# Two windowed-attention layers on one core: set-up cut into pieces with a semaphore each, and rel banks of 6, 4 and 4 image rows

## The chip, the cores and the metric

The kernel runs on one core of a Trainium2 chip. The time is the device time of one execution in microseconds (us). The engines are called as in the profile: PE (TensorE; PEld are its weight loads), DVE (VectorE), ACT (ScalarE), POOL (GpSimd) and SP (SyncE, whose queue SPq issues all transfers here).

## The reference

x is (64, 14, 14, 192). Two layers follow each other, each `x = x + attention(groupnorm(x))`, with 32 channel groups per sample and no affine part. Attention has 12 heads of 16 channels over the 196 tokens of a sample, with decomposed relative positions added to the scores:

```
attn = (q * 16**-0.5) @ k.T
attn[h, w, kh, kw] += q . Rh[h, kh] + q . Rw[w, kw]
out = softmax(attn) @ v @ proj_w + proj_b
```

Rh and Rw are rows of two tables of 27 x 16 per layer, picked by the difference of the two rows or columns of the image.

## The kernel before, in words

A unit is one sample of one layer; there are 128. Each engine runs the same loop of passes (`iteration`, line 500 for PE, 696 for DVE) with twelve slots each. A step of unit u is due at a fixed slot count after the unit's start (`JOBS`, lines 255 to 266, with the PSUM bank of each job), so up to nine units are in work at once: in each slot PE makes the row-maximum product of one head of one unit (line 511), the score product of one head of an older unit (line 524), and the jobs due there. All order within an engine is the order of this program, and engines meet through semaphores only. The passes are numbered i from -2; unit n has its step "at" in pass n + at // 12, slot at % 12.

The steps of a unit: the tile xa of a sample is loaded (line 386), PE transposes it (`xT`, line 421), ACT copies it, DVE takes channel statistics (line 726), PE sums them over groups with the matrix gmat (`g`, line 427), DVE copies the sums (line 771), POOL makes mean and rstd and the normalized xn, split into two half-precision parts xn_hi and xn_lo (lines 799 to 831). PE multiplies by split weights w_hi and w_lo (line 404) to q, k (`qk0`, `qk1`) and v (`v`). q and k go out to DRAM and come back in the layout of q_st and k_st.

The relative positions are extra rows of the contraction. k_st holds, in its rows 64 to 124, one-hot rows for image row, image column and a row of constants, the same for all heads and units (line 658 copies them head by head into six buffers). q_st gets, by transfer, the products of q with the tables (`rel0` to `rel2`, line 465). These are made for RELB = (6, 6, 2) image rows at a time, one PSUM bank for each: for each of 14 columns or rows i two small matmuls for the column axis, and for i below the number of image rows in the bank two more for the row axis. ACT writes the first part of each bank (line 619), DVE the rest (line 756). rel0 uses bank 0 in slot 5, rel1 bank 2 in slot 6, rel2 bank 2 in slot 8; V's product of another unit uses bank 2 in slot 9 and waits for rel2's reader on DVE (`bank_free`, line 289). After rel2, SP issues four transfers (line 355).

After the maxima of all heads (DVE, line 705), `mT` in slot 5 of a later pass turns them, ACT writes mrow, SP sends it to q_st (line 346), and the first score product needs it in slot 9. ACT takes the exponential (line 574). PE multiplies with V in groups of four heads, in slots 2, 5 and 8 (line 543); the group of slot 8 needs the exponential of the score product of the same slot. The rest (`ot`, `oT`, `y`) normalizes, projects and adds the residual (POOL, line 841).

Set-up: SP issues all constant transfers, then the weights of layer 0 and, after these are split, those of layer 1 through the same buffer w_raw (line 323). DVE fills pads (lines 643 to 651), makes the one-hot rows of all six k_st buffers, the pick table, the rel table rel_st, and scales and splits both layers' weights (lines 653 to 691). Then it signals s_setup; PE, ACT and POOL wait for that before their first instruction (lines 395, 553, 780).

Of the kernel before, what the change touches and what calls it, by code (L numbers as in the profile page):

```python
# [56 lines left out]
RELB = (6, 6, 2)  # L57
# [17 lines left out]
def attention_kernel(nc, x_in, w_all, b_qk, b_rows, rel, onehot, lo_rows, ident_in, gmat_in, out):  # L75
    with ExitStack() as ctx:
        def sb(name, shape, dt=F32):
            return ctx.enter_context(nc.sbuf_tensor(name, shape, dt))
# [19 lines left out]
        w_raw = sb("w_raw", [CB, 2, 4 * C])  # L98
# [59 lines left out]

        s_const = sem("s_const")
        s_wraw = sems("s_wraw", 2)  # L160
        s_pad = sem("s_pad")
        s_wsc = sem("s_wsc")
        s_bhi = sem("s_bhi")
        s_whi = sem("s_whi")
        s_wlo = sem("s_wlo")
        s_oh = sem("s_oh")
        s_setup = sem("s_setup")
# [143 lines left out]
        def _(sp):  # L311
            sp.dma_start(ident[:, :], ident_in).then_inc(s_const, 16)
            sp.dma_start(gmat[:, :], gmat_in).then_inc(s_const, 16)
            sp.dma_start(oh_raw[R_REL:STACK, :], onehot).then_inc(s_const, 16)
            sp.dma_start(is_lo[:, :], lo_rows).then_inc(s_const, 16)
            for part in range(2):
                sp.dma_start(b_raw[CC + part:CC + part + 1, :, :, :], b_qk.rearrange("(o n) l t -> o n l t", o=1))\
                  .then_inc(s_const, 16)
            for l in range(2):
                sp.dma_start(rel_in[2 * HD * l:2 * HD * l + 2 * HD, :, :, :],  # L320
                             rel[0:2 * HD].rearrange("(r d) l a n -> d r (l a n)", d=HD)).then_inc(s_const, 16)
            for layer in range(LAYERS):
                if layer:
                    sp.wait_ge(s_wlo, layer)
                sp.dma_start(w_raw[0:CC, :, :], w_all[layer].rearrange("(c p) n -> p c n", c=2))\
                  .then_inc(s_wraw[layer], 16)
# [14 lines left out]
            def iteration(unit, layer):  # L341
                for s in range(HEADS):
# [51 lines left out]
        def _(pe):  # L394
            pe.wait_ge(s_setup, 1)
            pe.wait_ge(s_const, 16 * 8)
# [12 lines left out]
            def job(name, unit, slot, layer):  # L409
# [14 lines left out]
                elif name == "g":  # L424
                    pe.wait_ge(s_mv, u.n + 1)
# [3 lines left out]
                elif name.startswith("qk"):  # L429
                    pe.wait_ge(s_xlo, u.n + 1)  # L430
# [68 lines left out]

            def iteration(unit, layer):  # L500
                for s in range(HEADS):
# [139 lines left out]
        def _(dve):  # L641

            nc.vector.memset(rel_raw[:, :, :, :], 0.0).then_inc(s_pad, 1)
            nc.vector.memset(halfpow[:, :], -0.5)
            nc.vector.memset(eps[:, :], EPS)
            nc.vector.memset(w_raw[CC:CB, 1, :], 0.0).then_inc(s_pad, 1)
# [3 lines left out]
            for i in range(VB):  # L650
                nc.vector.memset(v_st[i][:, :, :, :], VS)
            dve.wait_ge(s_const, 16 * 8)
            nc.vector.tensor_copy(oh_f16[R_REL:STACK, :].rearrange("p (k b r) -> p k r b", r=2, b=SIDE),
                                  oh_raw[R_REL:STACK, :].rearrange("p (k r b) -> p k r b", r=2, b=SIDE)).then_inc(s_oh, 1)
            dve.wait_ge(s_oh, 1)
            for i in range(QB):
                for head in range(HEADS):
                    nc.vector.tensor_copy(k_st[i][R_REL:STACK, head, :], oh_f16[R_REL:STACK, :])  # L658
            used = HG * (HD + 1)
            by_head = ident[:, :].rearrange("p (j x) -> p j x", x=PW)  # L660
            nc.vector.tensor_copy(pick[:, 0:used].rearrange("p (j x) -> p j x", j=HG), by_head[:, :, 0:HD + 1])
            nc.vector.tensor_copy(pick[:, used:128].rearrange("p (j x) -> p j x", j=HG), by_head[:, :, HD + 1:PW])
            dve.wait_ge(s_pad, 1)
            nc.vector.tensor_scalar(rel_raw[:, :, :, 0:2 * REL], rel_in[:, :, :, :], RS, None, ALU.mult)\
              .then_inc(s_wsc, 1)
            dve.wait_ge(s_wsc, 1)
            nc.vector.tensor_copy(rel_st[:, :, :, :], rel_raw[:, :, :, :]).then_inc(s_whi, 1)
            dve.wait_ge(s_whi, 1)
            nc.vector.tensor_scalar(rel_cut[:, :, :, :], rel_st[:, :, :, :], is_lo[0:64, 0:1], None, ALU.mult)\
              .then_inc(s_whi, 1)  # L670
            dve.wait_ge(s_whi, 2)
            nc.vector.tensor_tensor(rel_st[:, :, :, :], rel_raw[:, :, :, :], rel_cut[:, :, :, :], ALU.subtract)
            for layer in range(LAYERS):
                dve.wait_ge(s_wraw[layer], 16 * 3)
                dve.wait_ge(s_pad, 2)
                w_qk = w_raw[:, :, 0:2 * C].rearrange("p c (t x n) -> p c t x n", x=2, n=HQ * HD)
                for x, f in ((0, QS), (1, KS * HD ** -0.5)):
# [12 lines left out]
                nc.vector.tensor_tensor(w_hi[CC:CB, layer, 0, :], w_raw[CC:CB, 0, :], b_cut[CC:CB, :], ALU.subtract)  # L690
                nc.vector.tensor_tensor(w_lo[:, layer, :, :], w_raw[0:CC, :, :], w_hi[0:CC, layer, :, :],
                                        ALU.subtract).then_inc(s_wlo, 1)
            dve.wait_ge(s_wlo, LAYERS)
            nc.vector.memset(yo[0][:, :, :], 0.0).then_inc(s_setup, 1)

            def iteration(unit, layer):
                for s in range(HEADS):
# [69 lines left out]
                    if u:  # L767
# [5 lines left out]
                          .then_inc(s_g, 1)  # L773

# [4 lines left out]
        def _(pool):  # L779
            pool.wait_ge(s_setup, 1)  # L780
# [119 lines left out]
```

## Time and profile before

| | us |
|---|---|
| runs, median of 3 (lowest, highest) | 1896.43 (1894.51, 1898.62) |
| the profiled execution | 1894.12 |
| its span | 1892.3 |
| busy in the span: PE, DVE, ACT, POOL | 1807.1, 1401.2, 1352.2, 712.6 |

The profile is of one execution. A busy PE is not PE at its peak, for matmuls overlap. "[0.24 <-ACT x]" behind a row says that the engine was idle for 0.24 us before it and what released it. In a timeline equal neighbours are merged, with xN for their number.

### The profile page before, as it was taken

What the parts mean: (1) busy time and instruction counts of PE and PEld (TensorE: products, weight loads), DVE (VectorE), ACT (ScalarE), POOL (GpSimd) and SP (SyncE); (2) the same over time, 40 slices, a digit from 0 to 9 for tenths busy, and PEclk for the clock granted to TensorE, in tenths of its full rate; (3) what the DMA queues carried; (4) which work ended last, traced back from release to release, by engine and by line L of the source; (5) the groups of instructions that cost most, each with busy time, mean ns of one, the idle gap of its engine ahead of it and who ended that gap; (6) DMA issues with size and microseconds to landing.
All of it is one profiled execution on the core that took longest, in us unless ns stands there. A gap on an engine that the chain in (4) does not pass through costs nothing.

```text
span 1892.3 us, 84394 instructions
## 1 busy us (share of the span) xinstructions
PE 1807.1 (95%) x34176; PEld 1533.1 (81%) x34176; DVE 1401.2 (74%) x3568; ACT 1352.2 (71%) x3201; POOL 712.6 (38%) x1796
## 2 busy tenths in 40 slices
PE   0799999999999999999999999999999999999997
PEld 0688888888888888888888888888888888888885
DVE  6477777777777777777777777777777777777774
ACT  0277777777777777777777777777777777777776
POOL 1333443433433434334434334334344343343331
PEclk9999999999999999999999999999999999999999
DMA  1344444444444444444444444444444444444441
GB/s 36 95 105 108 104 113 111 102 115 107 107 110 107 111 109 106 114 108 104 113 110 104 113 108 109 109 106 112 109 106 113 110 103 111 110 104 113 108 104 33
DMA packets 142171, 197.76 MB, mean 105 GB/s; under 512 B 26455, under 2 KB 109656, under 8 KB 141786
## 3 DMA queue, kind: packets, MB, share of 16 engines
q1 hardware_dynamic: 141786, 192.36, 41.6%
q8 instruction: 274, 4.49, 1.0%
q14 instruction: 111, 0.91, 0.2%
HBM read 97.74 MB, written 57.80 MB: 82 GB/s over the span
## 4 chain that ended last, share of the span: by engine, by line
PE 86%; issue 4%; ACT 4%; DVE 2%; DMA 2%; SPq 1%; POOL 1%; POOLq 0%; ACTq 0%
PE ps_m L404 23%; PE ps_max L511 17%; PE ps_o L543 16%; PE ps_sc L524 13%; PE ps_m L465 8%; PE ps_m L479 4%; ACT probs L574 3%; PE ps_m L421 2%; PE ps_m L487 2%; DMA q_st<-mrow 1%; PE ps_m L470 1%; SPq L337 1%; PE ps_m L427 1%; DVE k_st L658 0%; POOL yo L841 0%
## 5 line engine op out<-in xcount | busy, mean ns | idle before, releaser
L705 DVE TENSOR_REDUCE mx<-ps_max 98x2 f32<-98x392 f32 x1536 | 828.9, 555 | 210.4 <-PE ps_max L511 210.1
L574 ACT ACTIVATE probs<-ps_sc 98x392 f32<-98x392 f32 x1536 | 722.9, 497 | 201.8 <-PE ps_sc L524 157.7
L511 PE MATMUL ps_max<-k_st,q_st 124*98 124x196 f16 x3072 | 536.6, 256 | 2.1 <-DVE mx L705 1.1
L524 PE MATMUL ps_sc<-q_st,k_st 125*98 125x196 f16 x3072 | 512.1, 248 | 3.7 <-DMA q_st<-mrow 2.7
L511 PEld LDWEIGHTS ps_max<-k_st,q_st 124*98 124x98 f16 x3072 | 292.1, 124 | 133.0 <-issue 80.3
L756 DVE TENSOR_TENSOR rel_hl<-ps_m,rel_hi 128x504 f16<-128x504 f32 (+1 forms) x384 | 217.2, 566 | 185.5 <-ACT rel_hi L619 185.4
L543 PE MATMUL ps_o<-probs,v_st 98*32 98x196 f32 x6144 | 335.7, 336 | 18.8 <-ACT probs L574 1.8
L524 PEld LDWEIGHTS ps_sc<-q_st,k_st 125*98 125x98 f16 x3072 | 320.7, 124 | 7.4 <-DMA q_st<-mrow 4.2
L799 POOL TENSOR_TENSOR msq<-gsm 96x2 f32<-96x2 f32 x128 | 24.3, 190 | 710.2 <-DVE gsm L771 710.2
L619 ACT ACTIVATE rel_hi<-ps_m,is_lo 128x504 f16<-128x504 f32 (+1 forms) x384 | 222.4, 579 | 33.4 <-PE ps_m L465 33.2
L465 PE MATMUL ps_m<-q_st,rel_st 64*32 64x36 f16 (+1 forms) x14336 | 237.9, 208 | 2.2 <-DVE rel_hl L756 1.6
L543 PEld LDWEIGHTS ps_o<-probs,v_st 98*32 98x32 f32 x6144 | 159.9, 109 | 93.6 <-ACT probs L574 32.0
L465 PEld LDWEIGHTS ps_m<-q_st,rel_st 64*32 64x32 f16 x14336 | 191.4, 101 | 54.4 <-DVE rel_hl L756 2.4
L404 PE MATMUL ps_m<-xn_hi,w_hi 98*128 98x196 f16 (+1 forms) x768 | 193.1, 251 | 4.7 <-POOL xn_lo L831 4.7
L404 PE MATMUL ps_m<-xn_lo,w_hi 96*128 96x196 f16 x768 | 192.0, 250 | 0.0
L404 PE MATMUL ps_m<-xn_hi,w_lo 96*128 96x196 f16 x768 | 191.4, 249 | 0.0
L563 ACT COPY o_sb<-ps_o 128x196 f32<-128x196 f32 x384 | 123.7, 322 | 80.3 <-PE ps_o L543 76.7
L789 POOL TENSOR_TENSOR msq<-mv 96x2 f32<-96x2 f32 x128 | 24.4, 190 | 341.0 <-DVE mv L731 341.0
L586 ACT CAST qk_hl<-ps_m 128x392 f16<-128x392 f32 (+1 forms) x256 | 103.3, 404 | 63.2 <-PE ps_m L404 63.2
L841 POOL TENSOR_TENSOR yo<-yr,xa 98x384 f32<-98x384 f32 x128 | 127.5, 996 | 54.0 <-ACT yr L633 54.0
L717 DVE TENSOR_TENSOR qk_hl<-ps_m,qk_hl 128x392 f16<-128x392 f32 (+1 forms) x256 | 117.0, 457 | 25.0 <-ACT qk_hl L586 11.4
L404 PE MATMUL ps_m<-w_hi,xn_hi 98*98 98x192 f16 (+1 forms) x512 | 127.7, 249 | 1.8 <-DVE rel_hl L756 1.7
(74 smaller groups left out, 2958.6 us busy)
## 6 DMA issues: line engine op xcount, KB each, us to landing
q_st<-q_dram SPq DMA_DIRECT2D x128, 294.0 KB, 3.9
k_st<-k_dram SPq DMA_DIRECT2D x256, 147.0 KB, 3.9
q_dram<-qk_hl SPq DMA_DIRECT2D x128, 147.0 KB, 2.9
k_dram<-qk_hl SPq DMA_DIRECT2D x128, 147.0 KB, 3.4
q_st<-rel_hl SPq DMA_DIRECT2D x256, 73.5 KB
q_st<-rel_hl SPq DMA_DIRECT2D x256, 64.3 KB
xa<-in_x SPq DMA_DIRECT2D x64, 147.0 KB
x<-yo SPq DMA_DIRECT2D x64, 147.0 KB
```

Of the source, the lines that this page charges most:

```text
L404: last = nc.tensor.matmul(dst, weights(a, c, k), moving(b, c, k), start=n == 0, stop=n == len(terms) - 1)
L465: last = nc.tensor.matmul(to, rel_st[:, lay, axis, w:w + RW], q, start=True, stop=True)
L511: last = nc.tensor.matmul(ps_max[head % 2][0:HT, h * TOK:h * TOK + TOK], q_st[u.n % QB][0:R_MAX, head, h, :], k_st[u.n % QB][0:R_MAX, head ...
L524: last = nc.tensor.matmul(ps_sc[head % 2][0:HT, kt * TOK:kt * TOK + TOK], k_st[u.n % QB][0:STACK, head, kt * HT:kt * HT + HT], q_st[u.n % ...
L543: last = nc.tensor.matmul(ps_o[32 * j:32 * j + 32, n * TOK:n * TOK + TOK], v_st[u.n % VB][:, kt, head_of(head), :], probs[head][:, kt, :], ...
L563: nc.scalar.copy(o_sb[u.r % 2][:, groups[0]:groups[-1] + 1, :] .rearrange("p g (k r b) -> p (g k) r b", r=2, b=SIDE), ps_o[:, 0:len(groups ...
L574: nc.scalar.activation(probs[head][:, :, :], ps_sc[head % 2][0:HT, 0:2 * TOK].rearrange("p (k t) -> p k t", k=2), ACT.Exp, scale=1.0 / (QS ...
L619: nc.scalar.activation(rel_part(rel_hi[u.r % 2], n), rel_bank(n), ACT.Identity, scale=is_lo[:, 0:1]).then_inc(s_rhi, 1)
L705: nc.vector.reduce_max(mx[u.r % 2][:, head, :], ps_max[head % 2][0:HT, 0:2 * TOK].rearrange("p (q k) -> p q k", q=2), axis=AX.X).then_inc( ...
L717: nc.vector.tensor_tensor(qk_hl[u.r % 2][:, 1, at, :], ps_m[BANK[f"qk{j}"]][:, 0:len(tiles) * TOK].rearrange("p (c t) -> p c t", t=TOK), q ...
L756: nc.vector.tensor_tensor(rel_part(rel_hl[u.r % 2], n), rel_bank(n), rel_part(rel_hi[u.r % 2], n), ALU.subtract).then_inc(s_rlo, 1)
L841: nc.gpsimd.tensor_tensor(yo[p2][:, :, :], yr[p2][:, :, :], xa[u.n % XB][:, :, :], ALU.add)\
```

## The change

- The constants are no longer behind one semaphore. SP issues the identity, then the first tile, then gmat, layer 0's weights and biases, the selector of low rows, the one-hot rows, the rel tables, and layer 1's weights into a buffer of their own. Only then comes the second tile.
- PE and ACT begin after the identity; each later reader waits for its own constant at its first use. POOL waits for nothing and now fills the pads of v_st (only the columns behind HD) and two small tables.
- Layer 0's weights are made on DVE in pass -1, slot 8, behind unit 0's statistics. The rel table and the one-hot rows of the first buffer are made in pass 0, slot 11; the pick table and the second buffer in pass 1, slot 11; the other four buffers in passes 2 to 5, slot 0. One instruction now writes all twelve heads of a buffer.
- Layer 1's weights are made in five pieces in passes 16 to 20, slot 1, each piece last in its slot on DVE.
- RELB is (6, 4, 4).

```diff
-RELB = (6, 6, 2)
+RELB = (6, 4, 4)
...
         @block.sync
...
+            sp.dma_start(ident[:, :], ident_in).then_inc(s_ident, 16)
+
+            def constants():
+
+                raw_weights(0)
+                for part in range(2):
+                    sp.dma_start(b_raw[CC + part:CC + part + 1, :, :, :], b_qk.rearrange("(o n) l t -> o n l t", o=1))\
+                      .then_inc(s_wraw[0], 16)
+                sp.dma_start(is_lo[:, :], lo_rows).then_inc(s_const, 16)
+                sp.dma_start(oh_raw[R_REL:STACK, :], onehot).then_inc(s_const, 16)
+                for l in range(2):
+                    sp.dma_start(rel_in[2 * HD * l:2 * HD * l + 2 * HD, :, :, :],
+                                 rel[0:2 * HD].rearrange("(r d) l a n -> d r (l a n)", d=HD)).then_inc(s_const, 16)
+                raw_weights(1)
...
                         sp.dma_start(xa[u.n % XB][:, :, :], tokens(src[bass.ds(at, 1)])).then_inc(s_x[u.r], 16)
+                        if u.n == 0:
+                            sp.dma_start(gmat[:, :], gmat_in).then_inc(s_gmat, 16)
+                            constants()
...
-            pe.wait_ge(s_setup, 1)
-            pe.wait_ge(s_const, 16 * 8)
+            pe.wait_ge(s_ident, 16)
...
+                    if u.n % SAMPLES == 0:
+                        pe.wait_ge(s_wlo, lay + 1)
...
+                        if u.n == 0:
+                            pe.wait_ge(s_rst, 1)
...
+                            if u.n < QB:
+                                pe.wait_ge(s_koh, u.n + 1)
...
-            act.wait_ge(s_setup, 1)
+            act.wait_ge(s_ident, 16)
...
+            def all_weights(layer):
+
+                dve.wait_ge(s_const, 16 * 4)
+                scale_weights(layer)
+                high_weights(layer)
+                low_bias(layer)
+                for c in range(2):
+                    low_weights(layer, c)
...
+            def one_hot(i):
+
+                dve.wait_ge(s_oh, 1)
+                nc.vector.tensor_copy(k_st[i][R_REL:STACK, :, :],
+                                      oh_f16[R_REL:STACK, :].rearrange("p (o t) -> p o t", o=1)
+                                      .to_broadcast([STACK - R_REL, HEADS, TOK])).then_inc(s_koh, 1)
...
+            def constants(i, s):
+
+                later = SAMPLES // 4
+                if (i, s) == (-1, 8):
+                    all_weights(0)
+                elif (i, s) == (0, HEADS - 1):
+                    rel_table()
+                    one_hot(0)
+                elif (i, s) == (1, HEADS - 1):
+                    pick_table()
+                    one_hot(1)
+                elif i in (2, 3, 4, 5) and s == 0:
+                    one_hot(i)
+                elif (i, s) == (later, 1):
+                    scale_weights(1)
+                elif (i, s) == (later + 1, 1):
+                    high_weights(1)
+                elif (i, s) == (later + 2, 1):
+                    low_bias(1)
+                elif i in (later + 3, later + 4) and s == 1:
+                    low_weights(1, i - later - 3)
...
+                    constants(unit(0).n, s)
...
-            pool.wait_ge(s_setup, 1)
+            nc.gpsimd.memset(halfpow[:, :], -0.5)
+            nc.gpsimd.memset(eps[:, :], EPS)
+            for i in range(VB):
+                last = nc.gpsimd.memset(v_st[i][:, :, :, HD:PW], VS)
+            last.then_inc(s_vpad, 1)
```

The functions scale_weights, high_weights, low_bias, low_weights, rel_table and pick_table hold the old instructions unchanged, except that the low weights are taken in two halves; raw_weights holds the three transfers of a layer's weights.

## Rows read from the trace of the kernel before

**Rows 1.** The page, its part on busy time: share of the span, instructions.

```profile
PE 1807.1 (95%) x34176; PEld 1533.1 (81%) x34176; DVE 1401.2 (74%) x3568; ACT 1352.2 (71%) x3201; POOL 712.6 (38%) x1796
```

**Rows 2.** Windows, one pass: stretch, length, busy us (instructions), clock, DMA.

```profile
602.35:616.40 14.05, 13.83 (x266) 11.57 (x265) 10.39 (x28) 10.25 (x25) 5.57 (x16) 1.00 0.45 109
```

**Rows 3.** Timeline of the head: start us, length, engine, line, tile, [idle before].

```profile
1.20 0.41 SPq L313 DMA_DIRECT2D gmat<-in_gmat  x1
...
3.89 4.74 DVE L651 MEMSET v_st<- 98x768 f32 x6 [0.20 <-issue]
...
9.06 8.95 DVE L658 COPY k_st<-oh_f 61x196 f16<-61x196 f16 x72
...
18.23 0.26 DVE L664 TENSOR_SCALAR rel_raw<-rel_in 64x216 f32<-64x216 f32 x1
...
19.51 0.35 DVE L678 TENSOR_SCALAR w_raw<-w_raw 96x384 f32<-96x384 f32 x1
...
21.68 0.96 DVE L685 CAST w_hi<-w_raw 98x1536 f16<-98x1536 f32 x1
...
24.29 1.75 DVE L691 TENSOR_TENSOR w_lo<-w_raw,w_hi 96x1536 f16<-96x1536 f32 x1
...
30.43 0.35 DVE L678 TENSOR_SCALAR w_raw<-w_raw 96x384 f32<-96x384 f32 x1 [4.39 <-DMA w_raw<-in_b_rows]
...
37.57 0.89 PE L421 MATMUL ps_m<-ident,xa 98*96 98x98 f32 x4 [37.57 <-DVE yo L694]
...
42.44 0.16 DVE L771 COPY gsm<-ps_m 96x4 f32<-96x4 f32 x1 [1.19 <-PE ps_m L427]
...
47.44 0.34 PE L404 MATMUL ps_m<-xn_hi,w_hi 98*128 98x196 f16 x1 [4.31 <-POOL xn_lo L831]
...
52.69 0.58 SPq L386 DMA_DIRECT2D xa<-in_x  x1
...
55.49 0.89 PE L421 MATMUL ps_m<-ident,xa 98*96 98x98 f32 x4 [2.52 <-DMA xa<-in_x]
```

**Rows 4.** Timeline of PE in a pass and its weight loads; the waits, 200 to 1800 us.

```profile
600.67 0.25 PE L404 MATMUL ps_m<-w_hi,xn_hi 98*98 98x192 f16 x1
...
610.36 0.67 PE L465 MATMUL ps_m<-q_st,rel_st 64*32 64x84 f16 x40
...
612.89 0.52 PE L465 MATMUL ps_m<-q_st,rel_st 64*32 64x84 f16 x32
...
606.61 0.20 PEld L511 LDWEIGHTS ps_max<-k_st,q_st 124*98 124x98 f16 x2
...
613.55 0.49 PEld L543 LDWEIGHTS ps_o<-probs,v_st 98*32 98x32 f32 x16 [0.24 <-ACT probs L574]
...
PEld ps_o L543 <- ACT probs L574: 27.0, 114, 0.2
...
PEld ps_sc L524 <- DMA q_st<-mrow: 3.0, 6, 0.6
```

**Rows 5.** Timeline of the same passes: DVE, then ScalarE (ACT), then POOL.

```profile
599.85 0.33 DVE L756 TENSOR_TENSOR rel_hl<-ps_m,rel_hi 128x168 f16<-128x168 f32 x1 [0.33 <-ACT rel_hi L619]
...
606.02 0.53 DVE L705 TENSOR_REDUCE mx<-ps_max 98x2 f32<-98x392 f32 x1
...
610.10 0.68 DVE L756 TENSOR_TENSOR rel_hl<-ps_m,rel_hi 128x504 f16<-128x504 f32 x1 [0.48 <-ACT rel_hi L619]
...
611.16 0.68 ACT L619 ACTIVATE rel_hi<-ps_m,is_lo 128x504 f16<-128x504 f32 x1 [0.20 <-PE ps_m L465]
...
613.47 0.40 ACT L619 ACTIVATE rel_hi<-ps_m,is_lo 128x168 f16<-128x168 f32 x1
...
606.60 1.00 POOL L841 TENSOR_TENSOR yo<-yr,xa 98x384 f32<-98x384 f32 x1
```

**Rows 6.** Timeline of the ramp: DVE, then PE.

```profile
67.76 0.63 DVE L726 BATCH_NORM_STATS2 bn<-xT 96x6 f32<-96x196 f32 x2 [3.48 <-ACT xT L608]
...
67.64 0.35 PE L404 MATMUL ps_m<-xn_hi,w_hi 98*128 98x196 f16 x1 [0.43 <-POOL xn_lo L831]
```

More of the change, by code:

```diff
@@ L97, in attention_kernel @@
         gmat = sb("gmat", [CC, CC])
-        w_raw = sb("w_raw", [CB, 2, 4 * C])
+        w_raw = [sb(f"w_raw{i}", [CB, 2, 4 * C]) for i in range(LAYERS)]
         w_hi = sb("w_hi", [CB, LAYERS, 2, 4 * C], F16)
@@ L156, in attention_kernel @@
         ps_m = [psum(f"ps_m{i}", [128, 512]) for i in range(3)]
+        s_ident = sem("s_ident")
+        s_gmat = sem("s_gmat")
         s_const = sem("s_const")
@@ L162, in attention_kernel @@
         s_wsc = sem("s_wsc")
+        s_whi = sem("s_whi")
         s_bhi = sem("s_bhi")
-        s_whi = sem("s_whi")
         s_wlo = sem("s_wlo")
+        s_rsc = sem("s_rsc")
+        s_rst = sem("s_rst")
         s_oh = sem("s_oh")
-        s_setup = sem("s_setup")
+        s_koh = sem("s_koh")
+        s_pick = sem("s_pick")
+        s_vpad = sem("s_vpad")
         s_x = sems("s_x")
@@ L311, in _, with raw_weights @@
         def _(sp):
[L312 to L325, printed above, removed]
+            def raw_weights(layer):
+                sp.dma_start(w_raw[layer][0:CC, :, :], w_all[layer].rearrange("(c p) n -> p c n", c=2))\
                   .then_inc(s_wraw[layer], 16)
@@ L328, in _ @@
                     p = CC + part
-                    sp.dma_start(w_raw[p:p + 1, 0, 2 * C:4 * C], b_rows[0:1, layer].rearrange("o b n -> o (b n)"))\
-                      .then_inc(s_wraw[layer], 16)
+                    sp.dma_start(w_raw[layer][p:p + 1, 0, 2 * C:4 * C],
+                                 b_rows[0:1, layer].rearrange("o b n -> o (b n)")).then_inc(s_wraw[layer], 16)
+            sp.dma_start(ident[:, :], ident_in).then_inc(s_ident, 16)
[10 more added lines that the diff above has]
+                raw_weights(1)
             def tokens(dram):
@@ L424, in job @@
                 elif name == "g":
+                    if u.n == 0:
+                        pe.wait_ge(s_gmat, 16)
                     pe.wait_ge(s_mv, u.n + 1)
@@ L446, in job @@
                     if n == 0:
+                        if u.n == 0:
+                            pe.wait_ge(s_rst, 1)
                         wait_dma(pe, s_qst, u)
@@ L472, in job @@
                 elif name == "ot":
+                    if u.n == 0:
+                        pe.wait_ge(s_pick, 1)
                     pe.wait_ge(s_o, u.n * len(PV) + len(PV))
@@ L535, in iteration @@
                             if i == 0:
+                                if u.n == 0:
+                                    pe.wait_ge(s_vpad, 1)
                                 wait(pe, s_v, u.n + 1)
@@ L614, in iteration @@
                         if u:
+                            if u.n == 0 and n == 0:
+                                act.wait_ge(s_const, 16 * 4)
                             act.wait_ge(s_rel_ps, u.n * 3 + n + 1)
@@ L641, in _ @@
         def _(dve):
[L643 to L646, printed above, removed]
             for i in range(2):
@@ L649, in _, with scale_weights @@
                 nc.vector.memset(oT_hi[i][CC:CB, :, :], 1.0)
[L650 to L676, printed above, removed]
+            nc.vector.memset(w_raw[0][CC:CB, 1, :], 0.0)
+            nc.vector.memset(w_raw[1][CC:CB, 1, :], 0.0)
+            nc.vector.memset(rel_raw[:, :, :, :], 0.0).then_inc(s_pad, 1)
+            def scale_weights(layer):
+                raw = w_raw[layer]
+                dve.wait_ge(s_wraw[layer], 16 * (5 if layer == 0 else 3))
+                dve.wait_ge(s_pad, 1)
+                w_qk = raw[:, :, 0:2 * C].rearrange("p c (t x n) -> p c t x n", x=2, n=HQ * HD)
                 for x, f in ((0, QS), (1, KS * HD ** -0.5)):
@@ L681, in _, with high_weights, low_bias @@
                                             .rearrange("p n t -> p t n"), f, None, ALU.mult).then_inc(s_wsc, 1)
-                nc.vector.tensor_scalar(w_raw[:, :, 2 * C:4 * C], w_raw[:, :, 2 * C:4 * C], VS, None, ALU.mult)\
+                nc.vector.tensor_scalar(raw[:, :, 2 * C:4 * C], raw[:, :, 2 * C:4 * C], VS, None, ALU.mult)\
                   .then_inc(s_wsc, 1)
-                dve.wait_ge(s_wsc, 1 + 5 * (layer + 1))
-                nc.vector.tensor_copy(w_hi[:, layer, :, :], w_raw[:, :, :]).then_inc(s_whi, 1)
-                dve.wait_ge(s_whi, 3 + layer)
+            def high_weights(layer):
+                dve.wait_ge(s_wsc, 5 * (layer + 1))
+                nc.vector.tensor_copy(w_hi[:, layer, :, :], w_raw[layer][:, :, :]).then_inc(s_whi, 1)
+            def low_bias(layer):
+                dve.wait_ge(s_whi, layer + 1)
                 nc.vector.tensor_scalar(b_cut[CC:CB, :], w_hi[CC:CB, layer, 0, :], is_lo[CC:CB, 0:1], None, ALU.mult)\
@@ L689, in _ @@
                 dve.wait_ge(s_bhi, layer + 1)
[L690 to L694, printed above, removed]
+                nc.vector.tensor_tensor(w_hi[CC:CB, layer, 0, :], w_raw[layer][CC:CB, 0, :], b_cut[CC:CB, :],
+                                        ALU.subtract)
@@ new lines, in low_weights @@
+            def low_weights(layer, c):
+                last = nc.vector.tensor_tensor(w_lo[:, layer, c, :], w_raw[layer][0:CC, c, :], w_hi[0:CC, layer, c, :],
+                                               ALU.subtract)
+                if c:
+                    last.then_inc(s_wlo, 1)
+            def all_weights(layer):
[5 more added lines that the diff above has]
+                    low_weights(layer, c)
@@ new lines, in rel_table @@
+            def rel_table():
+                dve.wait_ge(s_pad, 1)
+                nc.vector.tensor_scalar(rel_raw[:, :, :, 0:2 * REL], rel_in[:, :, :, :], RS, None, ALU.mult)\
+                  .then_inc(s_rsc, 1)
+                dve.wait_ge(s_rsc, 1)
+                nc.vector.tensor_copy(rel_st[:, :, :, :], rel_raw[:, :, :, :]).then_inc(s_rsc, 1)
+                dve.wait_ge(s_rsc, 2)
+                nc.vector.tensor_scalar(rel_cut[:, :, :, :], rel_st[:, :, :, :], is_lo[0:64, 0:1], None, ALU.mult)\
+                  .then_inc(s_rsc, 1)
+                dve.wait_ge(s_rsc, 3)
+                nc.vector.tensor_tensor(rel_st[:, :, :, :], rel_raw[:, :, :, :], rel_cut[:, :, :, :], ALU.subtract)\
+                  .then_inc(s_rst, 1)
+                nc.vector.tensor_copy(oh_f16[R_REL:STACK, :].rearrange("p (k b r) -> p k r b", r=2, b=SIDE),
+                                      oh_raw[R_REL:STACK, :].rearrange("p (k r b) -> p k r b", r=2, b=SIDE))\
+                  .then_inc(s_oh, 1)
@@ new lines, in one_hot, with pick_table @@
+            def one_hot(i):
[3 more added lines that the diff above has]
+                                      .to_broadcast([STACK - R_REL, HEADS, TOK])).then_inc(s_koh, 1)
+            def pick_table():
+                used = HG * (HD + 1)
+                by_head = ident[:, :].rearrange("p (j x) -> p j x", x=PW)
+                dve.wait_ge(s_ident, 16)
+                nc.vector.tensor_copy(pick[:, 0:used].rearrange("p (j x) -> p j x", j=HG), by_head[:, :, 0:HD + 1])
+                nc.vector.tensor_copy(pick[:, used:128].rearrange("p (j x) -> p j x", j=HG), by_head[:, :, HD + 1:PW])\
+                  .then_inc(s_pick, 1)
```

## The prediction

> **What bounds the kernel now.** I read the page first [rows 1]: TensorE (PE) is busy 95% of the span, so in the long middle only what PE waits for costs time. A window of one pass of twelve slots [rows 2] has 13.83 us of PE work in 14.05; such a stretch comes some 124 times (128 units, the first four in the ramp). So there are two targets: the head before the first product, and stalls inside a pass.
>
> The timeline of the head [rows 3] shows one chain: VectorE (DVE) works or waits for 37.5 us, then PE transposes the first tile at 37.57, and the first qk product is at 47.44. On the way DVE waits 4.39 for layer 1's raw weights, whose transfer had waited for layer 0's low weights.
>
> Inside a pass [rows 4] look at the products with V of slot 8. Their weight loads start at 613.55 with 0.24 idle before them, put down to the exponential; the waits view has that release 114 times, 27.0 us. The third rel bank in front of them, 32 matmuls in 0.52 us, is too short to cover the exponential of that slot: it ends at 612.89+0.52=613.41, 0.14 before.
>
> **The change, part by part.**
>
> *The head.* New order: identity, first tile, then the rest. The second issue stood at 1.20; a tile issued at 52.69 was used at 55.49, 2.8 us later [rows 3], so PE starts near 4.0 (bounds 3.8 and 5.5). From PE's 37.57 to the end of the group copy on DVE (42.44+0.16=42.60) it is 5.03 us: near 9.0. Of DVE's memsets six stood before 3.89, and a seventh is added, so DVE is free below 5 us, before it is asked. The V pads (4.74 us on DVE for whole tiles, half of each now) and the two small ones go to POOL, which has nothing to do before 8. Then DVE makes layer 0's weights: from 19.51 to 24.29+1.75=26.04, 6.5 us. Their transfers are issued between 2 and 6 us and layer 1's, issued at once after 26.04, took 4.39 [rows 3]: they land near 9 and cost nothing or some tenths. SP issues eleven set-up DMAs and three of layer 1 ahead of the second tile, 14 times some 0.4: it is issued near 8 and there by 11, ahead of its use at 15. PE, ACT and the queue of SP thus wait for single constants, and nothing is queued behind those waits that could run earlier. POOL's own path (from 42.60 to 47.4) is 4.8 us, ready at 13.8. The first qk product moves from 47.44 to 9.0+6.5+0.2=15.7: **-31.7**.
>
> *DVE and POOL side by side.* In the old head the two never worked at once for long. Now the weights on DVE lie beside unit 0's normalization on POOL (4.8 us, some 4.3 busy). The rel table (1.3, from 18.23 to 19.51), the one-hot's cast and the pick table (0.4 each) and two one-hots (1.6 by the next point), 3.7 together, lie beside the normalization of units 1 and 2, for which PE waits at once: 67.64, released by xn_lo [rows 6]. No row shows both engines on such operands: the bounds are 0 and full serial order, 4.3 + 3.7 = 8.0 us. No row is nearer to either end; I take half: **+4.0**. The Trainium skill (SBUF — State Buffer, Who interferes with whom) says that a DVE copy or tensor-scalar in a two-port mode, or a DVE instruction with two SBUF inputs, and a GpSimd instruction lock each other out whole. By that rule this term is near 8.0; that is a rival below, and no row here confirms it.
>
> *The one-hot rows.* 72 copies took 8.95 us [rows 3], 0.124 each; now there are six copies of twelve heads. Twelve old ones are 1.49 us, the upper end. One instruction pays its fixed part once: a cast of 1536 columns took 0.96, a copy of 2352 narrower elements should be near that or below; I take 0.8 (0.5 to 1.5). Those of units 0 to 2 fall in DVE's idle time (3.48 us a pass there [rows 6], more in the pass before); if that cover went, each costs 0.8. Those at passes 3 and 4 meet a DVE that waits for PE, some 0.1; at pass 5 the full 0.8: **+0.9** (0.3 to 2.4).
>
> *Layer 1's weights.* They go into passes 16 to 20, slot 1. There DVE has a queue: the slot 2 maximum ends at 606.02+0.53=606.55 [rows 5], and PE's load for slot 4, which waits for it, is at 606.61 [rows 4]. There is no slack, so each piece stalls PE whole. Pieces from the head's rows: 2.17 for the scaling (19.51 to 21.68), 0.99 for the cast, 1.62 for the bias rows, two halves of 1.75 with a fixed part, 0.92 each; 6.6, less 0.02 each: **+6.5** (3.3 to 6.6; below if DVE makes good half of it out of its 3.66 us idle a pass [rows 2]). Queued behind are the next maxima and qk's low part, all inside the same stall. POOL's y sum (1.00) and two small ones lie beside them [rows 5]: 0 to 5 x 1.4 = 7 by the unknown of the point before; mostly POOL will be the late one, and its results are not due: **+1.0**.
>
> *Rel banks 6, 4, 4.* 112 matmuls a unit as before: 40+36+36 for 40+40+32. The second bank gets four fewer. It is busy 0.67 for 40 matmuls against 0.52 for the 32 narrow ones [rows 4]; halfway is 0.595, so PE reaches slot 8 0.075 earlier (0 to 0.13). The third grows by the same, but under the exponential's wait, the 0.14 above. The mrow transfer, due in slot 9, has that much less time: in 6 of 114 units it is late already [rows 4], so 0.01 goes back. 0.065 x 124: **-8.1** (0 to -14). The readers: 504 columns take DVE 0.68, 168 columns 0.33, ScalarE 0.68 and 0.40 [rows 5]; for 336 halfway, 0.505 and 0.54. The third bank is free 0.14+0.17=0.31 later. V's product needs that bank: it was freed at 599.85+0.33=600.18 [rows 5] and used at 600.67 [rows 4], 0.49, less some 0.08 for its weight load. So 0.1 is left. In the ramp bank 1 gives back what bank 2 takes, and SP's rel transfers, 0.3 later, have ten slots.
>
> *Clock.* A qk matmul takes 0.34 at 47.44 [rows 3] against 0.25 at 600.67 [rows 4]: PE starts at the lower of its two levels (1.2 and 2.4 GHz). Where it rises may move: 0 forecast, 3 either way in the range.
>
> **The sum**: -31.7 + 4.0 + 0.9 + 6.5 + 1.0 - 8.1 = -27.4, from 1894.12 (span 1892.3 and 1.8 around it) to 1866.7. The median of the runs is 2.3 above the profiled execution, so I forecast **1869**.
>
> **Rivals.**
> 1. *No cost of sharing at all* (the old rows show none): -5.0, 1864. 0.15.
> 2. *Full exclusion of DVE and POOL* (for it: both use the same memory; against: no row): first product near 20, the next passes late, +4.0, and 3 more in passes 16 to 20: 1876. 0.15. It is the Trainium skill's rule named above.
> 3. *The bank split gives nothing*: a matmul of 24 columns costs like one of 36, or V's product eats the gain: 1877. 0.13.
> 4. *The head is not freed as it says*: tile or constants land late behind 1.3 MB of weights on one queue, and layer 0's weights start at 13 rather than 9: 1873. For it: one queue; against: the 4.39. 0.05.
> 5. *Slower*: V's product in slot 9 waits for the third bank in every pass. I have its readers 0.31 later with 0.4 to spare. Without the bank gain the rest is worth 19.3 us, 0.156 a pass, so this decides from 0.56 later on; at 0.65 it costs 0.25 x 124 = 31: 1896.4 - 19.3 + 31 = 1908. 336 columns would have to cost more than 504 did. 0.02.
>
> My forecast has 0.50. The range reaches from rival 1 with the full bank gain (1859) less 2 for the clock, to rival 2 with most of the bank gain gone: **1857 to 1882**. A measurement of this kernel tells about 0.2% (4 us) from no change: faster 0.97, same 0.01, slower 0.02.
>
> **What would show it.** First qk product at 15.7 (18 with sharing); the two xn ops of POOL longer than before where DVE has the weights; a pass of 13.98; the wait of the V products on the exponential down from 0.24; five stalls of PE at slot 4 in passes 16 to 20 of 2.2, 1.0, 1.6, 0.9 and 0.9; no wait of V's product on the third bank. A pass of 14.05 or more breaks the bank term, small stalls in passes 16 to 20 the layer 1 term.

## The result, and the profile after

| | before | after |
|---|---|---|
| runs, median (lowest, highest), us | 1896.06 (1894.51, 1898.62) | 1881.76 (1876.79, 1886.66) |
| profiled execution, its span | 1894.12, 1892.3 | 1882.77, 1881.0 |
| first qk product | 47.44 | 17.93 |
| median pass of twelve slots, from the starts of the maxima's transposes (mT) | 14.06 | 14.01 |

The ratio of the runs is 0.9925, interval [0.9913, 0.9938]: 14.3 us faster. The forecast was 27 us; the measured time lies just inside the slow end of the range, 1857 to 1882. The six executions of the changed kernel lie 10 us apart, and their mean granted clock goes from 0.994 (1878.69) and 0.993 (1876.79) down to 0.987 (1886.66); in the kernels of experiments 2 to 9 it is 0.995 to 0.999 in all executions but two.

The page has the same picture as [rows 1]. In a span 11 us shorter the busy times of PE, DVE, ACT and POOL rose all the same, PE's by 7 us:

```profile
PE 1814.0 (96%) x34176; PEld 1525.9 (81%) x34176; DVE 1407.1 (75%) x3496; ACT 1355.7 (72%) x3201; POOL 722.6 (38%) x1804
```

The head, as a timeline (start, length, engine, line, tile, idle before), answers to [rows 3]:

```profile
1.21 0.44 SPq L396 DMA_DIRECT2D xa<-in_x  x1
...
3.74 0.86 PE L433 MATMUL ps_m<-ident,xa 98*96 98x98 f32 x4 [3.74 <-DMA xa<-in_x]
...
8.58 0.16 DVE L850 COPY gsm<-ps_m 96x4 f32<-96x4 f32 x1 [1.18 <-PE ps_m L441]
...
10.24 0.35 DVE L683 TENSOR_SCALAR w_raw<-w_raw 96x384 f32<-96x384 f32 x1 [1.51 <-DMA rel_in<-in_rel]
...
10.94 1.18 POOL L902 TENSOR_SCALAR xn<-xT,nmean,rstd 96x196 f32<-96x196 f32 x2
...
13.11 1.52 POOL L915 TENSOR_TENSOR xn_lo<-xn,xn_hi 96x392 f16<-96x392 f32 x1
...
16.05 1.82 DVE L706 TENSOR_TENSOR w_lo<-w_raw,w_hi 96x768 f16<-96x768 f32 x2
...
17.93 0.34 PE L416 MATMUL ps_m<-xn_hi,w_hi 98*128 98x196 f16 x1 [4.91 <-DVE w_lo L706]
...
23.59 0.77 DVE L740 COPY k_st<-oh_f 61x2352 f16<-61x2352 f16 x1
```

PE starts at 3.74 and DVE's group copy ends at 8.74, as worked out (4.0 and 9.0). DVE then waits 1.51 for the rel tables, and its weights last from 10.24 to 17.87, 7.6 us instead of 6.5. On POOL the two xn ops took 1.18 and the low part 1.52, against 0.98 and 0.92 in the kernel before, where DVE stood idle beside them. The one-hot copy of twelve heads took 0.77.

From here the lead of after over before shrinks. At the first qk product it is 29.5 us, at unit 0's maxima transpose (the first) 27.8, at unit 2's 26.2, and it stays near that to pass 15 (26.4). Five passes follow, 16 to 20, of 18.27, 14.85, 18.10, 19.38 and 15.36 us, where before had 14.05 to 14.18: the lead falls from 26.4 to 10.8. From there to unit 120 it grows to 13.7, by the shorter passes, and the tail takes 2.4 back, most of it in units 124 to 126. That is the whole account of the profiled executions: 26.4 - 15.6 + 2.9 - 2.4 = 11.3, the difference of the two spans; the medians of the runs lie 14.3 apart.

Windows over those passes (stretch, length, busy us of PE, PEld, DVE, ACT and POOL, granted clock, DMA):

```profile
230.50:244.80 14.30, 11.61 (x210) 9.56 (x209) 11.20 (x29) 9.01 (x21) 5.65 (x14) 1.00 0.45 108
244.80:248.40 3.60, 3.60 (x58) 3.26 (x58) 2.25 (x6) 1.69 (x4) 0.00 (x0) 0.53 0.01 1
248.40:279.00 30.60, 27.07 (x504) 22.38 (x493) 23.55 (x55) 20.12 (x48) 11.98 (x28) 1.00 0.41 100
279.00:293.00 14.00, 14.00 (x200) 10.67 (x198) 6.02 (x13) 6.39 (x15) 4.24 (x11) 0.52 0.20 46
```

PE stands idle for 2.7 us of the first stretch and 3.5 of the third. Behind each of the two it is busy without a gap at a granted clock of about a half, 1.2 instead of 2.4 GHz; the clock's own records have this from 244.75 for 3.4 us and from 278.88 for 13.7 us.

The first of these idle times, with what DVE and POOL did (DVE, POOL, then PE):

```profile
241.42 0.32 DVE L683 TENSOR_SCALAR w_raw<-w_raw 96x384 f32<-96x384 f32 x1
...
242.18 1.09 DVE L683 TENSOR_SCALAR w_raw<-w_raw 96x384 f32<-96x384 f32 x1
...
243.71 0.56 DVE L687 TENSOR_SCALAR w_raw<-w_raw 98x768 f32<-98x768 f32 x1
244.19 0.56 DVE L784 TENSOR_REDUCE mx<-ps_max 98x2 f32<-98x392 f32 x1
```

```profile
242.06 0.99 POOL L925 TENSOR_TENSOR yo<-yr,xa 98x384 f32<-98x384 f32 x1
```

```profile
244.80 0.56 PE L533 MATMUL ps_max<-k_st,q_st 124*98 124x196 f16 x2 [2.56 <-DVE mx L784]
```

The scaling of layer 1's weights stands between two maxima. It should last 2.2 us; one of its ops took 1.09 instead of 0.35, and ends (243.27) only after POOL's y sum has ended (243.05). The slot 2 maximum comes 2.8 late and PE waits 2.56 for it.

Two passes later, at the bias rows, the same happens again (DVE, POOL, then PE):

```profile
275.70 1.78 DVE L701 TENSOR_TENSOR w_hi<-w_raw,b_cut 2x768 f16<-2x768 f32 x1
```

```profile
275.67 0.99 POOL L925 TENSOR_TENSOR yo<-yr,xa 98x384 f32<-98x384 f32 x1
```

```profile
278.11 0.37 PE L533 MATMUL ps_max<-k_st,q_st 124*98 124x196 f16 x2 [2.40 <-DVE mx L784]
```

The subtraction, 0.95 when POOL is idle, took 1.78 behind a y sum that started 0.03 before it, and PE waits 2.40. The fall of the clock at 278.88 is 0.8 behind the end of this wait.

A pass in the middle, PE first, then DVE and ACT, answers to [rows 4] and [rows 5]:

```profile
612.14 0.53 PE L483 MATMUL ps_m<-q_st,rel_st 64*32 64x84 f16 x36
...
614.55 0.53 PE L483 MATMUL ps_m<-q_st,rel_st 64*32 64x84 f16 x36
615.21 0.87 PE L567 MATMUL ps_o<-probs,v_st 98*32 98x196 f32 x16
...
616.22 0.33 PE L546 MATMUL ps_sc<-q_st,k_st 125*98 125x196 f16 x2
616.47 0.26 PE L416 MATMUL ps_m<-w_hi,xn_hi 98*98 98x192 f16 x1
```

```profile
615.81 0.51 DVE L835 TENSOR_TENSOR rel_hl<-ps_m,rel_hi 128x336 f16<-128x336 f32 x1 [0.76 <-ACT rel_hi L645]
```

```profile
615.24 0.54 ACT L645 ACTIVATE rel_hi<-ps_m,is_lo 128x336 f16<-128x336 f32 x1
```

The second bank, 36 matmuls, is busy 0.53: four fewer, and the 24-column ones cost what the 12-column ones did (32 in 0.52). The third is just as long, 0.53, and hidden. But V's product starts 0.25 behind the score product, where it was 0.17 (600.50 and 600.67 in the kernel before): its bank's reader on DVE ends at 616.32, and it starts 0.15 behind that.

PE's weight loads by releaser, 200 to 1800 us (us in total, times, longest), against [rows 4]:

```profile
PEld ps_max L533 <- DVE mx L784: 41.9, 114, 2.8
PEld ps_o L567 <- ACT probs L598: 26.4, 112, 0.2
...
PEld ps_sc L546 <- DMA q_st<-mrow: 6.1, 10, 1.1
```

The wait on the exponential did not shrink (0.24 each). The loads that wait for mrow went from 6 times and 3.0 us to 10 times and 6.1.

### The profile page after: what moved, and what is told of

It reads as the page before. It is cut to its first block, busy times and chain, and to the rows that moved or that the text cites. A ratio compares the mean times of both kernels' runs of the same rounds, so it can differ in the third digit from the quotient of the medians.

```text
span 1881.0 us, 84337 instructions
## 1 busy us (share of the span) xinstructions
PE 1814.0 (96%) x34176; PEld 1525.9 (81%) x34176; DVE 1407.1 (75%) x3496; ACT 1355.7 (72%) x3201; POOL 722.6 (38%) x1804
## 4 chain that ended last, share of the span: by engine, by line
PE 84%; issue 4%; ACT 4%; DMA 3%; DVE 2%; SPq 2%; POOL 1%; POOLq 0%; ACTq 0%
PE ps_m L416 23%; PE ps_max L533 16%; PE ps_o L567 15%; PE ps_sc L546 13%; PE ps_m L483 7%; PE ps_m L499 4%; ACT probs L598 3%; DMA q_st<-mrow 3%; PE ps_m L433 2%; PE ps_m L507 2%; PE ps_m L488 1%; SPq L347 1%; PE ps_m L441 1%; SPq L396 0%; POOL yo L925 0%
## 5 line engine op out<-in xcount | busy, mean ns | idle before, releaser
L835 DVE TENSOR_TENSOR rel_hl<-ps_m,rel_hi 128x336 f16<-128x336 f32 (+1 forms) x384 | 217.2, 566 | 212.0 <-ACT rel_hi L645 211.8
L645 ACT ACTIVATE rel_hi<-ps_m,is_lo 128x336 f16<-128x336 f32 (+1 forms) x384 | 222.8, 581 | 31.7 <-PE ps_m L483 10.6
L483 PE MATMUL ps_m<-q_st,rel_st 64*32 64x36 f16 (+2 forms) x14336 | 223.6, 207 | 1.6 <-DMA q_st<-q_dram 1.2
L483 PEld LDWEIGHTS ps_m<-q_st,rel_st 64*32 64x32 f16 x14336 | 177.3, 99 | 54.5 <-DMA q_st<-q_dram 2.6
L925 POOL TENSOR_TENSOR yo<-yr,xa 98x384 f32<-98x384 f32 x128 | 127.4, 995 | 56.9 <-ACT yr L659 56.9
```

Source lines behind the costliest of these rows:

```text
L483: last = nc.tensor.matmul(to, rel_st[:, lay, axis, w:w + RW], q, start=True, stop=True)
L645: nc.scalar.activation(rel_part(rel_hi[u.r % 2], n), rel_bank(n), ACT.Identity, scale=is_lo[:, 0:1]).then_inc(s_rhi, 1)
L835: nc.vector.tensor_tensor(rel_part(rel_hl[u.r % 2], n), rel_bank(n), rel_part(rel_hi[u.r % 2], n), ALU.subtract).then_inc(s_rlo, 1)
L925: nc.gpsimd.tensor_tensor(yo[p2][:, :, :], yr[p2][:, :, :], xa[u.n % XB][:, :, :], ALU.add)\
```

## The experiments

Each kernel was timed in five rounds beside the kernel before, whose medians there were 1896.99 (in one set of four) and 1896.11 (in the rest), so ratios are compared. Experiments 1, 3, 4 and 5 start from the changed kernel, 2 from the kernel before, 6 to 9 from the kernel of experiment 3. Theory A is that layer 1's weights in slot 1 lost the time, theory B that the banks did; the slot theory is A put more closely.

**1. The banks back.**

```diff
-RELB = (6, 4, 4)
+RELB = (6, 6, 2)
```

> The changed kernel with rel banks of 6, 6 and 2 rows again. Theory A (the bank split gives a small gain: in the changed kernel the second bank is 0.13 us shorter in every pass, and V's product in slot 9 gives 0.08 of it back by waiting for the third bank's reader): the undisturbed pass is 14.05 us again instead of 14.00, V's product no longer waits, and the time is 2 to 6 us above the changed kernel's 1881.8, near 1886. Theory B (the split is what lost the gain of the head, through V's product and the late mrow transfer): well below the changed kernel, under 1876.

Measured: 1890.46, ratio 0.9966 [0.9953, 0.9979]. The median pass is 14.06 again. This is 8.7 above the changed kernel, more than forecast: in its profile the passes 16 to 20 are even longer (18.63, 20.35, 17.39, 20.26, 14.89), with 17.1 and 13.7 us at half clock. So the split is a gain, and the difference to the changed kernel also holds some chance in the clock: its executions have a median granted clock of 0.989 against 0.9915, which makes some 4.7 of the 8.7 us (an estimate: 0.0025 of 1885). Theory B is out.

**2. The banks alone**, on the kernel before: (6, 6, 2) becomes (6, 4, 4).

> The kernel before with rel banks of 6, 4 and 4 rows and nothing else. Theory A: an undisturbed pass of 14.00 us, 0.05 x 124 = 6 us less, of which late mrow transfers take back some 2: 1892, ratio 0.998. Theory B: 1896 or more.

Measured: 1892.63, ratio 0.9980 [0.9971, 0.9988]: 4.4 us less. Median pass 14.01, and 12 of 90 passes (units 25 to 115) more than 0.05 longer, where there were 7. That is the gain of the split without layer 1's pieces. The clock is not quite out of it: the ramp in this profile has a half-clock stretch of 10.2 us, where the kernel before has one of 6.8.

**3. Layer 1's weights in eight pieces, in slot 5.**

```diff
-                elif (i, s) == (later, 1):
-                    scale_weights(1)
-                elif (i, s) == (later + 1, 1):
+                elif i in (later, later + 1, later + 2) and s == 5:
+                    scale_weights(1, (i - later,))
+                elif (i, s) == (later + 3, 5):
                     high_weights(1)
-                elif (i, s) == (later + 2, 1):
-                    low_bias(1)
-                elif i in (later + 3, later + 4) and s == 1:
-                    low_weights(1, i - later - 3)
+                elif i in (later + 4, later + 5) and s == 5:
+                    low_bias(1, (i - later - 4,))
+                elif i in (later + 6, later + 7) and s == 5:
+                    low_weights(1, i - later - 6)
```

> The changed kernel with layer 1's weights in eight pieces of at most one us, each in slot 5 of passes 16 to 23, where DVE waits for ScalarE and POOL is idle. Theory A (15.6 of the 18 us lost behind the head are lost in passes 16 to 20: PE waits at slot 4 for the slot 2 maximum, POOL's y sum stretches the pieces, and after the long waits PE runs at the lower clock): no pass above 14.1 there, no stretch at half clock, the time 1866 to 1868. Theory B (the loss comes from the banks or the ramp): 1878 or more.

Measured: 1865.08, ratio 0.9835 [0.9822, 0.9847], 16.7 us below the changed kernel. The passes 16 to 23 last 14.00 to 14.19. The window over pass 16 to 20:

```profile
230.00:300.00 70.00, 69.37 (x1337) 58.69 (x1336) 56.45 (x141) 52.70 (x126) 27.82 (x70) 1.00 0.45 110
```

PE is busy 69.4 of 70 us, clock 1.00. Theory A.

**4. The same eight pieces in slot 1** (5 becomes 1 in the four conditions).

> The same eight pieces, but in slot 1 of passes 16 to 23. If a piece costs its length wherever DVE has a queue, and the clock falls only after a long wait: eight waits of 0.5 to 1.2 us, together 7 to 9, no stretch at half clock there, 1874 to 1876. If the clock falls for short waits too: 1881 or more, with half-clock stretches in 240 to 360 us. If slot 1 has slack after all: as e3_eight_slot5.

Measured: 1871.56, ratio 0.9867 [0.9852, 0.9881], 2.4 us below the range forecast. Eight passes lose 0.78, 0.78, 0.50, 0.84, 1.40, 1.08, 0.84 and 0.84, together 7.0 us, and the clock stays up:

```profile
240.00:270.00 30.00, 28.61 (x542) 23.82 (x538) 23.53 (x60) 21.62 (x51) 11.54 (x30) 1.00 0.47 115
270.00:300.00 30.00, 28.39 (x536) 23.48 (x534) 22.99 (x56) 21.46 (x51) 12.07 (x29) 1.00 0.43 107
300.00:330.00 30.00, 28.21 (x535) 23.48 (x534) 23.66 (x58) 21.40 (x51) 12.27 (x28) 1.00 0.40 97
330.00:360.00 30.00, 28.53 (x541) 24.05 (x542) 23.62 (x59) 21.68 (x51) 12.59 (x31) 1.00 0.43 107
```

So slot 1 costs each piece nearly its length (6.6 for all), as forecast; some 0.5 of the pass that lost 1.40 is a wait for mrow. PE's own idle times at the eight pieces are 0.24 to 0.88, and none of them lowered the clock. In the changed kernel the same work cost 15.9 over five median passes. Of the other 9, 1.6 are what the y sum added to two DVE ops (0.73 and 0.83), and the rest, some 7, goes to the clock: an estimate, for 17.1 us at half clock can cost at most 8.5. Experiment 5 has the long pieces without the y sum.

**5. The five whole pieces in slot 5** (1 becomes 5 in the changed kernel's conditions).

> The changed kernel with layer 1's five pieces whole (the scaling is 2.2 us long), only moved from slot 1 to slot 5 of passes 16 to 20. Slot theory (DVE's free time after slot 5, some 1.1 us with what the double buffers allow, covers a piece, and POOL is idle so that the scaling keeps its 2.2 us): waits of 1.1 us for the scaling, 0.5 for the bias rows, none for the rest, no stretch at half clock in 240 to 300 us: 1866 to 1868. Size theory (the long piece is what lowers the clock, wherever it is): half-clock stretches again and 1873 or more.

Measured: 1866.37, ratio 0.9843 [0.9830, 0.9857]. DVE and PE's weight loads in pass 16:

```profile
244.81 0.35 DVE L683 TENSOR_SCALAR w_raw<-w_raw 96x384 f32<-96x384 f32 x1
...
245.60 0.36 DVE L683 TENSOR_SCALAR w_raw<-w_raw 96x384 f32<-96x384 f32 x1
...
246.40 0.56 DVE L687 TENSOR_SCALAR w_raw<-w_raw 98x768 f32<-98x768 f32 x1
```

```profile
247.49 0.17 PEld L533 LDWEIGHTS ps_max<-k_st,q_st 124*98 124x98 f16 x2 [1.01 <-DVE mx L784]
```

Away from POOL's y sum the two scaling ops take 0.35 and 0.36, and the bias rows' subtraction 0.95. PE's weight load waits 1.01, three passes lose 1.1, 0.8 and 0.8, and the clock stays at 1.00. The second of these three, the cast's pass, holds a wait of 0.65 for mrow and none for DVE. The slot theory holds; the low weights and the cast are free there, as forecast, the bias rows cost 0.8 rather than 0.5.

**6. Layer 0's weights not behind the rel tables.**

```diff
             def constants():
 
+                sp.dma_start(is_lo[:, :], lo_rows).then_inc(s_wraw[0], 16)
                 raw_weights(0)
...
-                sp.dma_start(is_lo[:, :], lo_rows).then_inc(s_const, 16)
...
             def all_weights(layer):
 
-                dve.wait_ge(s_const, 16 * 4)
                 scale_weights(layer)
```

The readers of the other constants wait for them where they read.

> Eight pieces in slot 5, and layer 0's weights wait only for their own transfers and the low-row selector, not for the rel tables and one-hot rows. In the changed kernel DVE waited 1.51 us for the rel tables' transfer. If that wait is the whole of it: weights start 1.5 us earlier and the first qk product is at 15.9 instead of 17.4, 1863.5 against 1865.1. If the selector and the weights land no earlier than the rel tables did, or POOL's normalization shares more with the weights: first product at 17 or later, the same time.

Measured: 1864.92, ratio 0.9835 [0.9821, 0.9848]: nothing gained. The transfers were there, and DVE's weights ran from 8.78 to 15.62. In the profile of experiment 3 they ran from 9.53 to 17.30: that execution waited only 0.64 for the rel tables, not 1.51, so the wait that could be gained there was smaller than the expectation has it. DVE, POOL and PE:

```profile
8.78 0.36 DVE L686 TENSOR_SCALAR w_raw<-w_raw 96x384 f32<-96x384 f32 x1
...
13.65 1.97 DVE L712 TENSOR_TENSOR w_lo<-w_raw,w_hi 96x768 f16<-96x768 f32 x2
```

```profile
11.95 2.87 POOL L908 TENSOR_SCALAR xn<-xT,nmean,rstd 96x196 f32<-96x196 f32 x2
...
16.21 0.92 POOL L921 TENSOR_TENSOR xn_lo<-xn,xn_hi 96x392 f16<-96x392 f32 x1
```

```profile
17.28 0.32 PE L416 MATMUL ps_m<-xn_hi,w_hi 98*128 98x196 f16 x1 [4.28 <-POOL xn_lo L921]
```

POOL's two xn ops now took 2.87 (0.98 alone, 2.05 in experiment 3), and the first product, at 17.28 (17.36 in experiment 3), is released by POOL. What DVE gained, POOL lost.

**7. V's product one slot later.**

```diff
-                (9, "v", 2, (s_v, 1, 1)),
+                (10, "v", 2, (s_v, 1, 1)),
```

> Eight pieces in slot 5, and V's product one slot later (slot 10), so that the third rel bank's reader has one slot more. If V's product does wait for that reader in every pass (its first matmul stands 0.163 us behind the one before it, where it was 0.084): a pass of 13.93 us instead of 14.01, 124 x 0.08 = 10 us less, 1856. If the 0.08 are something else, or a new wait takes its place (scores of slots 9 and 10 now stand side by side, ScalarE takes 0.44 each): a pass of 14.01 and 1865.

Measured: 1855.23, ratio 0.9786 [0.9772, 0.9799]; median pass 13.92. The 0.08 were the wait for the third bank's reader. Mean pass (units 25 to 115) 13.99: 17 of 90 are more than 0.05 longer, by 5.8 us in all; PE's loads wait for mrow 13 times, 5.7 us. The profiled execution is the slowest of the four (1858.61), and it holds 10.2 us at half clock from 1807.6, right behind a PE wait of 1.34 for a transfer.

**8. The tile issued behind mrow.**

```diff
-        SP_AT = {"m": 41, "rel": 19, "qk_out": 3, "q_in": 9, "k_in": 9, "out": 72, "xa": -21}
+        SP_AT = {"m": 41, "rel": 19, "qk_out": 3, "q_in": 9, "k_in": 9, "out": 72, "xa": -18}
```

> Eight pieces in slot 5, and the tile of a later unit is issued in slot 6 instead of slot 3, behind the mrow transfer on SP instead of ahead of it. If late mrow transfers (13 of 90 passes are over 0.05 us longer, 3.9 us in all) come from SP's queue, mrow is issued 0.6 us earlier and they vanish: mean pass 14.01 instead of 14.05, 1861. If they come from the DMA engines' own load: unchanged, 1865.

Measured: 1858.20, ratio 0.9805 [0.9792, 0.9818]; mean pass 14.03, four late ones. That is 6.9 us below experiment 3, where 4 were forecast; the profiled executions lie 4.6 apart, 2.5 of it in units 25 to 115, and the rest is not accounted for. SP's queue in this kernel and in that of experiment 3:

```profile
606.99 0.83 SPq L356 DMA_DIRECT2D q_st<-mrow  x1
607.87 1.45 SPq L396 DMA_DIRECT2D xa<-in_x  x1
```

```profile
607.16 0.59 SPq L396 DMA_DIRECT2D xa<-in_x  x1
607.79 0.84 SPq L356 DMA_DIRECT2D q_st<-mrow  x1
```

mrow is issued 0.04 after the issue of k's transfer has ended (606.95) instead of 0.68 (607.11), and PE's waits for it are gone from the waits view. They came from the queue.

**9. The three edits together** (3, 7 and 8).

> The three edits that gained, together: layer 1's weights in eight pieces in slot 5, V's product in slot 10, the tile issued in slot 6. If they are independent: 1865.1 - 9.9 - 6.9 = 1848, a median pass of 13.92 and a mean within 0.03 of it. If the shorter pass takes back what the earlier mrow transfer gave (the transfer's time does not shrink with the pass): 1852 to 1855, mean pass 13.96 or more.

Measured: 1848.24, ratio 0.9754 [0.9740, 0.9767]: faster than both kernels, by 47.9 and 33.5 us. Median pass 13.92, mean 13.93. Of PE's weight loads, those of the row maxima and of V's products wait as before; for mrow they wait no more, and for q 0.5 us in all:

```profile
PEld ps_o L567 <- ACT probs L598: 27.1, 115, 0.2
...
PEld ps_m L483 <- DMA q_st<-q_dram: 0.5, 2, 0.2
```

## Why the prediction was right or wrong

- **The head**: right. Forecast -31.7 + 4.0 + 0.9 = -26.8, measured -26.2 by unit 2. Within it the first product stands at 17.93 for 15.7 + 2.2. "They land near 9 and cost nothing or some tenths" was wrong by 1.5 us of wait for the rel tables (0.64 in experiment 3's profile). The first product stands at 17.93 with the wait of 1.51, at 17.36 with 0.64 and at 17.28 with none (experiment 6), so at most 0.65 hung on it: POOL's share takes its place.
- **DVE and POOL side by side**: half of full exclusion was taken, for lack of a row. The traces show ops waiting for each other: in experiment 6 POOL took 2.87 for 0.98 beside the weights, and in the changed kernel DVE took 1.09 for 0.35 in pass 16 and 1.78 for 0.95 in pass 18, both times beside a y sum that had started first and kept its 0.99. The Trainium skill's rule (SBUF — State Buffer, Who interferes with whom) agrees with these numbers. That the first product nevertheless came at 17.93 and not at 20 fits with POOL's small ops (96x2) finding room beside DVE's; that was not measured by itself.
- **The one-hot rows**: 0.77 measured, 0.8 taken. The Trainium skill (VectorE: DVE Perf Modes, The perf-mode tier table) gives 693 ns for a copy of 2048 bf16 elements; by proportion, an estimate, 2352 of two bytes take 0.80, and the trace agrees.
- **Layer 1's weights**: the step that failed. "So each piece stalls PE whole", +6.5, is what experiment 4 measured for pieces of at most one us, 7.0. The changed kernel paid 15.9. In its place the runs showed two further costs. POOL's y sum made the scaling 0.73 and the bias rows 0.83 longer, 1.6 in all. I had +1.0 for this and said that mostly POOL would be the late one, which was wrong in these two: the y sums, 0.12 and 0.03 ahead, kept their 0.99, and DVE waited. And behind the two PE idle times, of 2.56 and 2.40, the granted clock fell to the lower level for 3.4 and 13.7 us. This is the larger part, and the sum has no term for it: I had the clock only in the head, as 3 us either way; of the 17 us at half clock up to 8.5 are lost. The trace of before could have warned: at 91 to 98 us it has one such stretch.
- **The banks**: -8.1 forecast; -4.4 in experiment 2. The gain in the second bank was 0.13, the upper bound, not 0.075: 24 columns cost no more than 12. "So 0.1 is left" was wrong: V's product waits 0.08. The reader's two ops grew by the 0.31 worked out (0.54 and 0.51), but the reader also starts later, at 615.24, 0.03 behind the products with V and not 0.08 ahead of them; and from its end to V's first matmul it is 0.15, not 0.08. Why ScalarE starts later is open: before, it began 0.06 behind the end of the bank's matmuls, now 0.16, and by the profile the bank ends 0.07 to 0.09 before the exponential does in both. Experiment 7 takes the wait away and gets the 0.08. So it was my third rival in a mild form. The mrow transfer cost a little more than 0.01 a pass (0.02 in the mean), and experiment 8 shows it as SP's queue.
- **"The wait of the V products on the exponential down from 0.24"**: wrong. The third bank did not grow in time, so it covers no more than before; the gain came from the second bank alone.
- The slower rival had the right place, V's product, but 0.25 us a pass where 0.08 was measured.
- **The tail**: the sum has no term for it, and it cost 2.4. The changed kernel has there a PE wait of 1.16 for a transfer of q and 3.4 us at half clock.
- That the time lies inside the range is in part luck: 0.24 us more and it would not. The slow end was built from full exclusion of DVE and POOL with most of the bank gain gone. Measured were the head as forecast, half of the bank gain, and layer 1's weights at 8 us over the forecast, of which the second rival had 3.

What stays open: why the clock fell for 13.7 us behind the third piece and 3.4 behind the first, and why the ramp holds a half-clock stretch of 10.2 us in the changed kernel and 6.8 in the others with the same head. Lone stretches without a piece of the weights stand in the changed kernel (1835.4, 3.4 us), in experiment 6 (768.9, 3.4 us) and in experiment 7 (1807.6, 10.2 us). Each came behind a PE wait for a transfer, of 1.16, 1.01 and 1.34; but waits of 1.30 and 1.09, in experiments 4 and 3, were not followed by one. In the changed kernel and in experiments 7 and 4, PE:

```profile
1833.22 0.67 PE L483 MATMUL ps_m<-q_st,rel_st 64*32 64x84 f16 x40 [1.16 <-DMA q_st<-q_dram]
```

```profile
1806.55 0.66 PE L483 MATMUL ps_m<-q_st,rel_st 64*32 64x84 f16 x40 [1.34 <-DMA q_st<-q_dram]
```

```profile
1824.26 0.67 PE L483 MATMUL ps_m<-q_st,rel_st 64*32 64x84 f16 x40 [1.30 <-DMA q_st<-q_dram]
```

No run varied the length of a wait by itself.

## What to carry to other kernels

Set-up work that is moved out of the head into a loop is priced by the slot it lands in: look for the engine's idle time right after its last due op there, cut the pieces to it, and see which other engine works at that moment (here POOL, whose sums held DVE up twice). A wait of PE costs its length, and it can cost as much again through the clock: here behind each of four waits of 2.4 to 2.6 us, and behind three of five of 1.0 to 1.4. When a bank is freed later, add not only the readers' longer ops but their later start and the step to the next product.

## What the runs showed of the hardware that I had not expected

- A DVE scaling of 96 x 384 took 0.35 alone and 1.09 beside a POOL sum of 0.99, a DVE subtraction of 2 x 768 took 0.95 alone and 1.78 beside the same sum; POOL's two xn ops took 0.98 alone, 1.18 to 2.87 beside DVE's weights.
- In the profiles of the two kernels and the nine experiments PE had, between 100 and 1836 us, nine idle times of 1.0 us or more. Behind seven of them the granted clock went to its half, at the latest 2.2 us after their end, for 3.4 to 17.1 us: 2.56 and 2.40 in the changed kernel and again in experiment 1, 1.34, 1.16 and 1.01. Behind 1.30 and 1.09 it stayed. Nowhere else in that time did it fall.
- In the head the matmuls tell the clock and the windows view does not. In the changed kernel a qk matmul takes 0.34 to 0.37 up to 56.9 us, as it does in the later stretch at half clock, and 0.25 right behind 57.1. But the trace's clock records begin at 57.0, and the view prints 1.00 for what lies before.
- A small matmul of 64 rows and 32 columns of weights costs about the same with 12 and with 24 moving columns: a bank of 28 such matmuls of 24 columns and 8 of 84 was busy 0.53, one of 28 of 12 columns and 4 of 84 was busy 0.52, one of 28 of 36 columns and 12 of 84 was busy 0.67 [rows 4]. Whether the 36 columns or the four more of 84 make that difference was not separated.
